# Transformer layers on one core: weights copied ahead of exponentials, a unit turned behind the queries, sums of squares ahead of the maxima

## What is computed

```python
def _layer(x, wqkv, qs, ksc, wo, lg, lb, w1, b1, w2, b2):   # 8 heads of 64, windows of 128 rows
    h = shift_token(x)                                      # half of the columns one row later
    q, k, v = jnp.split(h @ wqkv, 3, axis=-1)
    q = l2norm(q) * qs
    k = l2norm(k) * ksc
    q, k = rotary_xpos(q, k)
    o = local_attention(q, k, v)                            # softmax over this window and the one before
    x = x + o @ wo
    h = shift_token(x)
    h = (h - mean) / sqrt(var + 1e-05) * lg + lb
    a, g = jnp.split(h @ w1 + b1, 2, axis=-1)
    x = x + (a * gelu(g)) @ w2 + b2
    return x
```

## Time and profile before

| | |
|---|---|
| median of 3 runs | 4214.67 us (4213.24 to 4216.29) |
| profiled execution, its own time | 4225.78 us |
| its span | 4223.9 us |
| mean granted TensorE clock | 0.954 |
| busy: PE, VectorE, ScalarE, POOL | 90%, 73%, 62%, 45% |
| layers, in the span | about 1480 to 2790 us and 2850 to 4224 us |

### The profile page before, as it was taken

The page is one execution under the profiler, slowest core; times in us unless marked ns, Lnnn a source line. Parts: engine busy times, 40 slices in busy tenths (PEclk is TensorE's granted clock), DMA queues, the critical chain, the costliest instruction groups (busy, mean ns, idle before and its releaser), DMA issues. The chain is left out here.

```text
span 4223.9 us, 88004 instructions
## 1 busy us (share of the span) xinstructions
PE 3783.4 (90%) x33070; PEld 2915.1 (69%) x33070; DVE 3073.9 (73%) x7221; ACT 2616.6 (62%) x5752; POOL 1883.9 (45%) x1453
## 2 busy tenths in 40 slices
PE   4899999999998569999999999976999999999997
PEld 2454544545444358888888888865888888888886
DVE  5577777777776367777877877736788788788884
ACT  1455555555554357777777777745777777777774
POOL 1212322322332135555555555533665656656664
PEclk7799999999998779999999999987999999999998
DMA  4334254244341110000000000001000000000000
GB/s 128 86 67 119 64 115 117 54 111 104 71 122 43 38 57 14 20 19 15 20 17 17 19 15 20 12 28 55 22 26 22 26 23 27 26 23 24 23 24 21
DMA packets 145443, 195.93 MB, mean 46 GB/s; under 512 B 21532, under 2 KB 119544, under 8 KB 145024
## 3 DMA queue, kind: packets, MB, share of 16 engines
q1 hardware_dynamic: 145024, 190.31, 17.6%
HBM read 113.66 MB, written 67.16 MB: 43 GB/s over the span
## 5 line engine op out<-in xcount | busy, mean ns | idle before, releaser
L728 ACT ACTIVATE a_e_t<-a_ring 128x1024 f32<-128x1024 f32 (+3 forms) x768 | 610.9, 809 | 530.3 <-PE a_ring L869 367.7
L1050 DVE TENSOR_REDUCE a_mx<-a_ring 128x2 f32<-128x1024 f32 (+3 forms) x768 | 724.6, 956 | 236.9 <-PE a_ring L869 118.7
L1624 POOL TENSOR_TENSOR b_e<-b_e,b_share 128x512 f32<-128x512 f32 (+1 forms) x512 | 503.9, 987 | 792.3 <-DVE b_share L2072 791.9
L1730 ACT ACTIVATE b_e<-b_e,b_bias 128x256 f32<-128x256 f32 (+1 forms) x1024 | 494.2, 486 | 155.2 <-DVE b_bias L2064 154.2
L2064 DVE CUSTOM_DVE_ANT_0 b_e<-b_bank_s,b_mask,b_inv 128x256 f32<-128x256 f32 (+1 forms) x1024 | 415.8, 460 | 42.3 <-PE b_bank_s L1898 42.3
L1609 POOL TENSOR_TENSOR b_qk_rot<-b_qk_rot,b_rot 128x512 f32<-128x512 f32 x256 | 350.1, 1377 | 142.5 <-DVE b_rot L2037 142.5
L1740 ACT ACTIVATE b_e_t<-b_bank_et 128x512 f32<-128x512 f32 (+1 forms) x512 | 287.3, 561 | 200.5 <-PE b_bank_et L1909 200.1
L882 PE MATMUL a_ring<-a_k_st,a_q_st 48*128 48x512 f32 (+3 forms) x1536 | 330.1, 427 | 78.3 <-ACT a_e_t L728 41.6
L907 PE MATMUL a_ring<-a_q_st,a_k_st 50*128 50x512 f32 (+3 forms) x1536 | 341.0, 442 | 35.9 <-ACT a_e_t L728 13.2
L907 PEld LDWEIGHTS a_ring<-a_q_st,a_k_st 50*128 50x128 f32 x1536 | 147.7, 189 | 296.3 <-issue 147.5
L1909 PE MATMUL b_bank_et<-b_ident,b_e 128*128 128x128 f32 x1920 | 311.4, 282 | 44.9 <-ACT b_e_t L1740 44.9
(11 more groups left out here) (237 smaller groups left out, 11057.5 us busy)
## 6 DMA issues: line engine op xcount, KB each, us to landing
a_q_st<-a_parts_q SPq DMA_DIRECT2D x192, 128.0 KB, 4.7
a_k_st<-a_parts_k SPq DMA_DIRECT2D x192, 128.0 KB, 7.4
a_parts_q<-a_qk_p SPq DMA_DIRECT2D x16, 1024.0 KB, 8.0
a_parts_k<-a_qk_p SPq DMA_DIRECT2D x16, 1024.0 KB, 8.2
b_fl<-f_rows SPq DMA_DIRECT2D x64, 256.0 KB, 4.1
a_xl<-in_L_attn_x SPq DMA_DIRECT2D x9, 1024.0 KB, 5.3
a_x<-in_L_attn_x SPq DMA_DIRECT2D x8, 1024.0 KB, 8.5
x_rows<-a_x SPq DMA_DIRECT2D x8, 1024.0 KB, 4.6
```

The source lines that it names most:

```text
L728: act.activation(e_t[:, step % 2, 2 * pair:2 * pair + 2, 0:cols], slot[:, :].rearrange("p (h t) -> p h t", h=2)[:, :, 0:cols], ACT.Exp).th ...
L1050: dve.reduce_max(mx[:, g % 2, :, pair, piece, t:t + 1], slot[:, :].rearrange("p (r c) -> p r c", r=2)[:, :, 0:cols], AX.X)\
L1624: pool.tensor_tensor(weights, weights, share[:, h % SPS, 2 * j:2 * j + 2].unsqueeze(2) .broadcast_to([P, 2, 2 * WIN - lo]), ALU.mult).then ...
L1730: ins = act.activation(weights, weights, ACT.Exp, scale=-1.0, bias=bias[:, h % SPS, at:at + 1], accum_out=total[:, h % SPS, at:at + 1])
```

## The change

Four edits to the order of calls, in the layer stage alone. No instruction is added, removed or resized.

1. ScalarE: in the fourth half step, `take_turned(before, 0)` goes ahead of `exponentials(h, 0)`, as it does already in the first and third; only in the second (`late`) does it stay behind.
2. PE: `turn_unit` goes behind `project("q", w)`.
3. VectorE: in the third half step `sum_squares` goes ahead of `row_tops`, and `nearer_norms` ahead of `shares(h, 0)`. This holds where `sums_first` is true, that is where `frame.unit(g, W2_AT)` exists.
4. To follow the third, `inverse_norms` goes ahead of `exponentials(h, 0)` on ScalarE, and `scale_k` between the two `share_out` on POOL.

```diff
@@ POOL
+                    share_out(g, 0)
+                w, sums_first = frame.window(g, ROTATE_AT), frame.unit(g, W2_AT) is not None
+                if w is not None and sums_first:
+                    scale_k(w)
+                if frame.half(g) is not None:
+                    share_out(g, 1)
...
@@ ScalarE
-                if before is not None and g % SPW == 0:
+                late = g % (SPW * UNIT) == 1
+                if before is not None and not late:
                     take_turned(before, 0)
+                w = frame.window(g, ROTATE_AT)
+                sums_first = frame.unit(g, W2_AT) is not None
+                if w is not None and sums_first:
+                    inverse_norms(w)
                 if h is not None:
                     exponentials(h, 0)
-                if before is not None and g % SPW:
+                if before is not None and late:
                     take_turned(before, 0)
@@ TensorE
-                u = frame.unit(g, NORM_AT)
-                if u is not None:
-                    turn_unit(u)
                 w = frame.window(g, PROJECT_AT)
...
                     project("q", w)
+                u = frame.unit(g, NORM_AT)
+                if u is not None:
+                    turn_unit(u)
@@ VectorE
+                h, w = frame.half(g), frame.window(g, ROTATE_AT)
+                sums_first = frame.unit(g, W2_AT) is not None
+                if w is not None and sums_first:
+                    sum_squares(w)
                 if h is not None:
                     row_tops(h)
...
+                if w is not None and sums_first:
+                    nearer_norms(w)
                 if h is not None:
                     shares(h, 0)
```

More of the change, by code:

```diff
@@ L1655, in _ @@
                 if frame.half(g) is not None:
-                    for j in range(PPS):
-                        share_out(g, j)
+                    share_out(g, 0)
[4 more added lines that the diff above has]
+                    share_out(g, 1)
                 u = frame.unit(g, NORM_AT)
@@ L1664, in _ @@
                 w = frame.window(g, ROTATE_AT)
-                if w is not None:
+                if w is not None and not sums_first:
                     scale_k(w)
@@ L2159, in _ @@
                     add_unit(u)
-                h = frame.half(g)
+                h, w = frame.half(g), frame.window(g, ROTATE_AT)
+                sums_first = frame.unit(g, W2_AT) is not None
+                if w is not None and sums_first:
+                    sum_squares(w)
                 if h is not None:
@@ L2168, in _ @@
                     key_lo(turn)
+                if w is not None and sums_first:
+                    nearer_norms(w)
                 if h is not None:
                     shares(h, 0)
-                w = frame.window(g, ROTATE_AT)
-                if w is not None:
+                if w is not None and not sums_first:
                     sum_squares(w)
```

## The result

| | |
|---|---|
| before | 4213.95 us, median of 4 runs (4206.35 to 4216.29) |
| changed | 4334.31 us, median of 4 runs (4332.1 to 4336.91) |
| ratio | 1.029, 95% interval 1.027 to 1.031: slower |
| profiled execution of the changed kernel | 4333.32 us, span 4331.5 us, mean granted clock 0.946 |

A forecast was written before the change was run, and what follows sets the result against it. It took a loop of PE, VectorE and the `b_hs` transfer as the bound. Loop 71 us plus clock falls 46 us made 117 us, 4343 us from the profiled execution, 4332 us at the median; range 4275 to 4370 us.

The forecast's parts named there:

- The loop: Each period is a PE part and a VectorE part with the `b_hs` transfer; early sums lengthen it by 1.41 us.
- the sum: Cost over 58 periods: 71 us for the longer loop plus 46 us for clock falls, 117 us in all.
- The clamp at the border of two POOL instructions: In the third half step the sums' clamp slips in between two POOL instructions and takes 0.26 us.
- rival B: The clamp waits for POOL's `b_hid_lo`; loop 3.0 us longer per period, clock falls each time, 4481 us; chance 0.04.
- The stall moves from the turned weights to the output projection: PE's wait for the copy goes; PE waits about 2.1 us per period for `b_o_lo` at the output projection instead.
- a sign of being wrong: No PE wait for `b_o_lo`, listed among the observations that would show the forecast wrong.
- The 0.18 us of slack: Gain per period at the output projection from the earlier copy and later unit, 10 us over 58 periods.
- The wait for the unit: PE reaches the normed unit some 0.3 us before it is ready, in each period of the changed kernel.
- The clock: PE's 2.1 us wait lowers the clock in half of the 58 periods, 1.6 us each, 46 us.
- Rival A: The clock stays up and only the longer loop costs, 71 us: 4286 us; chance 0.24.
- C: A shorter transfer landing hides the shift of `add_attention`; 4204 us if below 3.7 us; chance 0.06, split between faster and same.

The follow-up runs named there:

- The sums put back: The changed kernel with `sum_squares` back in its old place, so edits 1 and 2 alone: 4213.16 us, 0.999 of the kernel before.
- `add_attention` ahead of the maxima: Edits 1 and 2 with the sums in their old place and `add_attention` ahead of `row_tops` in the third half step: 4164.85 us, 0.986 of the kernel before.
- `add_attention` first: The changed kernel, sums still early, with `add_attention` ahead of sums and maxima in the third half step: 4268.83 us, 1.011 of the kernel before.
- the keys' low part first: The changed kernel with `key_lo` ahead of the maxima in the fourth half step: 4304.84 us, 1.019 of the kernel before.
- queries twice: The changed kernel with the queries' projection done twice in each fourth half step, same result: 4308.97 us, 1.021 of the kernel before.
- the sums alone: Edits 3 and 4 alone, without edits 1 and 2: 4309.24 us, 1.022 of the kernel before.

## Why the prediction was right, and where it was off

- **The loop and where the sums stand in it: right.** The loop grew by 71 to 73 us where the sum had 71. The sums put back takes all of it away, and `add_attention` ahead of the maxima turns it into a gain. The maxima of the third half step start 1.39 us later (predicted 1.41), the clamp took 0.24 us (0.26), and VectorE's idle time before the moments is 2.2 us (2.2).
- **The clamp at the border of two POOL instructions: right.** It slips in, and rival B did not come. It came in the run with `add_attention` first, where the clamp reached its start 0.16 us behind POOL's next instruction in place of 0.16 us ahead of it, and took 1.70 us. The Trainium skill's rule that whoever issues first holds the shared port for a whole instruction ("SBUF — State Buffer", Who interferes with whom) agrees with both.
- **"The stall moves from the turned weights to the output projection": wrong place.** PE waits for `b_o_lo` in none of the 58 periods of the changed kernel, and the prediction had named that as a sign of being wrong. I followed PE's operands and not its banks. The keys' projection writes bank `b_bank_t`, which `key_lo` reads out first, and `key_lo` stands behind the maxima as `values_lo` does. PE waits there 1.72 us. The trace of before had shown how near it was: 0.32 us, where the shift is 1.41. The output projection follows 0.05 us behind `b_o_lo` all the same, so that the sum was not touched: with the keys' low part first, the wait is where I had put it, and the loop is the same.
- **The 0.18 us of slack: right in size, half of it lost again.** With the sums put back, the output projection starts 0.05 us behind `b_o_lo` (2014.21 behind 2013.48 + 0.68) in place of 0.24, but the periods are only 0.08 us shorter. From the first product of the output projection to the next scores it takes 1.61 us in that run and in the changed kernel (2126.67 to 2128.28), where it took 1.51 us before, when PE came to it without a wait. So edits 1 and 2 bring 5 us, not 10.
- **The wait for the unit: mis-sized.** 0.3 us was predicted, 0.8 us in the mean of nine was measured (7.4 / 9). It lies ahead of the long wait, which is shorter for it.
- **The clock: right in kind, near in size, by a weaker argument than the runs give.** "Half of the 58 periods" were 31, with 28 falls in them. A period with slow time costs 1.31 us and not 1.6: at the low clock products of 512 columns start 0.43 us apart in place of 0.23, and of 256 columns 0.22 in place of 0.11, less than double in part, and some stretches begin inside the wait, where nothing runs. That makes 41 to 43 us in place of 46. But I drew it from the length of one wait, 2.1 us, and counted four such waits. The ends of the layers in the trace of before had more: the fall at 2787.3 came behind two waits, of 2.04 and 0.49 us, and a pair of only 1.02 and 0.49 us had a fall behind it in the second layer (4145.8) and none in the first (near 2770).
- **What decides whether the clock falls stays open.** The length of one wait does not do it alone. In the changed kernel PE waits 1.72 us for `b_k_lo` in all 58 periods, nearly always with a wait for the unit ahead of it, and the clock fell 28 times. A wait of 1.72 to 1.74 us without one for the unit ahead was followed by a fall 3 times of 13 (queries twice) and 4 of 15 (`add_attention` ahead of the sums). That fits two waits with little between them, but a lone wait does it too where it is longer: the sums alone have 25 falls. Nor is length without a part: no wait under 1.59 us had a fall behind it in the 58 periods of any run, and the keys' low part first has none over 1.56 us.
- **Rival A** (clock up, 4286 us) is the loop without the falls, a ratio of 1.017. The keys' low part first is nearest to it: no falls, a loop 8 to 10 us longer than that of the changed kernel, and 1.019. **C** would need a shorter transfer; it took 4.95 us on the chain. The Trainium skill gives its 2.0 us ("DMA: Bandwidth & Descriptors", Anatomy of one DMA) for transfers that GpSimd issues, which the prediction left out; this one is issued by SyncE. At 2.0 us, by the working of rival C, the move would have been hidden; the trace after says again that it isn't so for this transfer.

The spans of the two profiled executions differ by 107.6 us: the 58 periods by 113.4, less some 6 us in the first attention, which the change doesn't touch. The medians differ by 120 us, since the profiled execution of before was 12 us above its median and that of after on it. The sum was made against the former's span and then moved by 11 us to the median; so the forecast of 4332 us rests on 117 us of cost where the periods show 113, and the nearness to 4334 is in part luck. That the falls came in half of the periods, a share taken from four waits, was luck too.

## What to carry to other kernels

When a transfer closes a loop between two engines, what is put in front of its issue is paid in full, and what stands behind it is free until it lands, unless it delays another way to the same engine: put the instruction that feeds it first, and any work that can wait behind it. A stall of PE for a late operand is not a gain to be had; follow the chain behind the operand to the next one that it makes late, banks that must be read out among them. And when waits can't be avoided, count the falls of the clock in the trace: in the one run here with dense products between the two waits there were none, though the longer wait was also a little shorter.

## What the runs showed of the hardware

- Falls of the clock in 58 periods, with PE's waits in the fourth half step: none with 0.4 and 0.6 us (before); 3 with one wait of 1.3 us in the mean (queries twice), all three behind waits of 1.7 us; 25 with one of 2.2 us (the sums alone); 28 with 0.8 and 1.7 us and eight transposes between them (the changed kernel); none with 0.8 and 1.55 us and the keys' projection between them. One wait of 1.55 us in the mean in the third half step (`add_attention` first) had 7.
- PE work of 1.4 us added to each period made the kernel faster (1.021 against 1.029), because it lay in a wait and left 3 falls of 28.
- The same clamp of 16 columns took 0.24 us in the changed kernel and 1.70 us with `add_attention` first, by a start that shifted 0.3 us against that of POOL's next instruction; in both it is so in every such period.
